# Attention's running state in half the columns, its products on quarters of the array, and one reciprocal square root for two layer norms, in a fused FFN, linear attention and FFN kernel

## The reference

```python
def _L0_attn_ref(x, Wqkv, bqkv, Wout, bout, gamma, beta):      # x is layer-normed
    q, k, v = jnp.split(x @ Wqkv.T + bqkv, 3, axis=-1)         # 16 heads of 16
    q = (jax.nn.elu(q) + 1.0 + FEAT_EPS) / jnp.sqrt(jnp.asarray(E, q.dtype))
    k = jax.nn.elu(k) + 1.0 + FEAT_EPS
    kv_cumsum = jnp.cumsum(jnp.einsum('blhe,blhf->blhef', k, v), axis=1)
    k_cumsum = jnp.cumsum(k, axis=1)
    num = jnp.einsum('blhe,blhef->blhf', q, kv_cumsum)
    den = jnp.einsum('blhe,blhe->blh', q, k_cumsum)[..., None] + FEAT_EPS
    out = (num / den).reshape(B, L, D) @ Wout.T + bout
    mu, var = jnp.mean(out, -1, keepdims=True), jnp.var(out, -1, keepdims=True)
    return (out - mu) / jnp.sqrt(var + LN_EPS) * gamma + beta
...
x = x + 0.5 * _L0_ffn_ref(_layernorm(x), w_gate, w_up, w_down)
x = x + _L0_attn_ref(_layernorm(x), ...)
x = x + 0.5 * _L0_ffn_ref(_layernorm(x), w_gate, w_up, w_down)
```

## Time and profile before

| | us |
|---|---|
| median of 3 runs (2298.89 to 2307.05) | 2300.2 |
| the profiled execution | 2303.45 |
| its span, first to last instruction | 2301.4 |
| PE busy, in the span | 2168.6 (94%) |
| DVE busy | 2135.8 (93%) |
| POOL busy | 1981.5 (86%) |
| ACT busy | 1853.5 (81%) |
| the causal mask of the first tile starts, that of the last | 802.2, 1560.4 |

### The profile page before, as it was taken

The page is one execution under the profiler, slowest core; times in us unless marked ns, Lnnn a source line. Parts: engine busy times, 40 slices in busy tenths (PEclk is TensorE's granted clock), DMA queues, the critical chain, the costliest instruction groups (busy, mean ns, idle before and its releaser), DMA issues.

```text
span 2301.4 us, 84889 instructions
## 1 busy us (share of the span) xinstructions
PE 2168.6 (94%) x27362; PEld 1558.6 (68%) x27362; DVE 2135.8 (93%) x5237; ACT 1853.5 (81%) x3878; POOL 1981.5 (86%) x3241
## 2 busy tenths in 40 slices
PE   0599999999999899999999999996999999999998
PEld 0356666666666689888889988883666666656665
DVE  8889999999999789999999999997999999999997
ACT  2778888888888678888888888877888888888885
POOL 1689999999999789998999999987989899899996
PEclk9899999999999999999999999998999999999999
DMA  3265555555554433333333333332544444444445
GB/s 93 54 125 111 118 111 117 112 116 112 116 115 97 87 63 69 69 68 67 68 69 66 69 68 68 67 66 46 109 116 112 110 115 111 115 112 108 117 111 118
DMA packets 733441, 216.28 MB, mean 94 GB/s; under 512 B 664774, under 2 KB 733126, under 8 KB 733382
## 3 DMA queue, kind: packets, MB, share of 16 engines
q1 hardware_dynamic: 733382, 215.57, 43.2%
HBM read 20.38 MB, written 16.78 MB: 16 GB/s over the span
## 4 chain that ended last, share of the span: by engine, by line
PE 39%; DVE 37%; issue 9%; POOL 8%; DVEq 2%; DMA 1%; SPq 1%; ACT 1%; POOLq 0%; ACTq 0%
DVE ffn_y L566 10%; DVE ffn_per_block L535 8%; PE attn_ps_qk L1068 7%; DVE ffn_hx L528 6%; PE ffn_ps_gu L676 6%; PE attn_ps_sc L1107 6%; POOL ffn_h_hl L609 3%; PE attn_ps_z L1129 3%; DVE ffn_q L562 3%; PE ffn_ps_down L688 3%; PE attn_ps_kT_v L1075 3%; PE attn_ps_num L1091 3%; PE attn_ps_num L1097 3%; POOL ffn_h_hl L608 3%; PE attn_ps_kv L1119 2%
## 5 line engine op out<-in xcount | busy, mean ns | idle before, releaser
L676 PE MATMUL ffn_ps_gu<-wgu_hi,ffn_xT 128*128 128x512 f16 (+1 forms) x3072 | 738.0, 363 | 32.7 <-DMA ffn_xT<-ffn_x_hl 32.7
L676 PEld LDWEIGHTS ffn_ps_gu<-wgu_hi,ffn_xT 128*128 128x128 f16 x3072 | 301.0, 98 | 319.2 <-issue 30.9
L676 PE MATMUL ffn_ps_gu<-wgu_lo,ffn_xT 128*128 128x512 f16 (+1 forms) x1536 | 431.9, 363 | 0.0
L624 ACT ACTIVATE ffn_quarter<-ffn_y,offsets 128x960 int16<-128x960 f32 (+2 forms) x264 | 282.6, 1071 | 172.9 <-DVE ffn_y L566 172.0
L688 PE MATMUL ffn_ps_down<-wd_hi,ffn_hT 128*128 128x256 f16 x2816 | 350.9, 273 | 19.9 <-DVE x_sb L555 13.9
L608 POOL TENSOR_TENSOR ffn_h_hl<-ffn_q,ffn_h_scale_hi 128x704 f16<-128x704 f16 x256 | 351.2, 1372 | 13.8 <-issue 6.3
L609 POOL TENSOR_TENSOR ffn_h_hl<-ffn_q,ffn_h_scale_lo 128x704 f16<-128x704 f16 x256 | 354.0, 1383 | 0.0
L688 PEld LDWEIGHTS ffn_ps_down<-wd_hi,ffn_hT 128*128 128x128 f16 x2816 | 265.5, 98 | 100.6 <-issue 36.9
L535 DVE TENSOR_REDUCE ffn_per_block<-ffn_hx 128x60 f32<-128x960 f32 (+2 forms) x264 | 298.5, 1131 | 22.7 <-ACT ffn_hx L660 0.3
L566 DVE TENSOR_TENSOR ffn_y<-ffn_hx,ffn_per_block 128x960 f32<-128x960 f32 (+2 forms) x264 | 295.4, 1119 | 0.0
L658 ACT ACTIVATE ffn_odd<-ffn_quarter,offsets 128x960 f16<-128x960 int16 (+2 forms) x264 | 278.6, 1055 | 5.5 <-POOL ffn_shift L601 5.5
(11 more groups left out here) (170 smaller groups left out, 5365.9 us busy)
## 6 DMA issues: line engine op xcount, KB each, us to landing
attn_v_eo<-attn_v_nat SPq DMA_DIRECT2D x512, 34.0 KB, 1.9
x_sb<-in_L_attn_x SPq DMA_DIRECT2D x128, 128.0 KB, 2.2
out<-x_sb SPq DMA_DIRECT2D x128, 128.0 KB, 1.8
ffn_xT<-ffn_x_hl SPq DMA_TRANSPOSE x256, 2.4
ffn_hT<-ffn_h_hl SPq DMA_TRANSPOSE x256, 3.5
attn_xT<-attn_x_hl SPq DMA_TRANSPOSE x128
attn_oT<-attn_o_hl SPq DMA_TRANSPOSE x128, 2.4
x_sb<-in_L_ffn_w_gate SPq DMA_DIRECT2D x1, 704.0 KB
```

What stands on the lines that cost most here:

```text
L624: nc.scalar.activation(quarter[:, back], y[:, back], ACT.Identity, bias=offsets[:, 0:1], scale=4.0 / HALF_MIN).then_inc(S["quarter"], 1)
L676: last = nc.tensor.matmul(ps_gu[par][:, a:b], xT[par][:, c, :], w[:, k, a:b], start=(n == 0), stop=(n == len(terms) - 1))
```

## The change

Five things change, all in attention.

1. **State.** The raw state is computed per 64 columns of k (g = 0, 1) with only the four heads of v that belong to them. Four heads' 17 columns stand in a row, 68 for each c, so `first`, `second`, `mid` and `before` have 136 columns where they had 272. `own` is the mask for that.
2. **PE's products.** q times state is done as 64x64 pieces of the array over 68 columns, after the products of the scores with v. The scores are done as 64x64 pieces too, twice as many with half the output rows. `ps_num` takes two banks (heads in the order of g), and the banks for k's transposes and v also hold the two raw states.
3. **Order on PE and ACT.** The transposes of k stand behind q and k's projection, and `k_nat` on ACT behind the exponential. The waits that this takes are new: v waits for `v_nat` and `second`, the raw state for `v_nat` of the next tile, `ps_num` for k's spread form and q's rows, which only the scores waited for.
4. **One square root.** The variances of x and z stand in one tile, so one addition and one power of two columns replace two of each. On POOL beta's sum and `shift` change places.
5. **Small.** o's scale goes into `den`, so `o` is a plain product of two tensors. The setup has 3 loads more on SP (`wout` in 4 pieces), and three small instructions more.

```diff
+        first, second = sb("first", [P, DC, PAIRS, VW]), sb("second", [P, DC, PAIRS, VW])
...
-        ps_kT_v = psum("ps_kT_v", [P, 512])
+        ps_kT_first = psum("ps_kT_first", [P, 512])
...
-        ps_kv = psum("ps_kv", [P, 2, 512])
-        ps_num = psum("ps_num", [P, HEADS, VW])
+        ps_v_second = psum("ps_v_second", [P, 512])
+        ps_num = psum("ps_num", [P, 2, 512])
...
-            return ps_kv[:, s, 0:HEADS * VW].rearrange("p (h w) -> p h w", w=VW)
+            return (ps_kT_first, ps_v_second)[s][:, D:D + WIDE]
...
-                nc.vector.tensor_scalar(den[:], ps_num[:, :, E], 4.0 * FEAT_EPS, None, ALU.add).then_inc(S["den"], 1)
+                nc.vector.tensor_scalar(den[:].rearrange("p (g h) -> p g h", g=2), num[:, :, :, E], 4.0 * FEAT_EPS, o_scale[:, 2:3], ALU.add, ALU.mult).then_inc(S["den"], 1)
...
-                nc.vector.scalar_tensor_tensor(o[:].rearrange("p (h e) -> p h e", e=E), ps_num[:, :, 0:E], o_scale[:, 0:1],
-                                               rden[:].unsqueeze(2).to_broadcast([P, HEADS, E]), ALU.mult, ALU.mult).then_inc(S["o_ready"], 1)
+                nc.vector.tensor_tensor(o[:].rearrange("p (g h e) -> p g h e", g=2, e=E), num[:, :, :, 0:E],
+                                        rden[:].rearrange("p (g h) -> p g h", g=2).unsqueeze(3).to_broadcast([P, 2, HEADS // 2, E]), ALU.mult).then_inc(S["o_ready"], 1)
...
-                ready(pool, "stats", tn)
-                freed(pool, "xn", tn, 2)
-                nc.gpsimd.tensor_tensor(rstd[oth][:], mv[oth][:, 1:2], eps[:], ALU.add).then_inc(S["var"], 1)
...
             if valid(tn, N):
-                ready(pool, "var", tn)
-                nc.gpsimd.tensor_tensor(rstd[oth][:], rstd[oth][:], minus_half[:], ALU.pow).then_inc(S["rstd"], 1)
+                ready(pool, "stats", tn)
+                freed(pool, "xn", tn, 2)
             if valid(tz, N):
                 ready(pool, "z_stats", tz)
                 if not (isinstance(tz, int) and tz < 2):
                     pool.wait_ge(attn_added, tz - 1)
+            if valid(tn, N) or valid(tz, N):
+                nc.gpsimd.tensor_tensor(rstd[oth][:, both], mv[oth][:].rearrange("p (s two) -> p s two", two=2)[:, both, 1], eps2[:, both], ALU.add).then_inc(S["var"], 1)
+                pool.wait_ge(S["var"], i + 4)
+                nc.gpsimd.tensor_tensor(rstd[oth][:, both], rstd[oth][:, both], minus_half[:, both], ALU.pow).then_inc(S["rstd"], 1)
             if valid(tn, N):
-                ready(pool, "rstd", tn)
-            if valid(tz, N):
-                nc.gpsimd.tensor_tensor(z_rstd[oth][:], z_mv[oth][:, 1:2], z_eps[:], ALU.add).then_inc(S["z_var"], 1)
-            if valid(tn, N):
-                nc.gpsimd.tensor_scalar(shift[oth][:], mv[oth][:, 0:1], -1.0, rstd[oth][:], ALU.mult, ALU.mult).then_inc(S["shift"], 1)
+                pool.wait_ge(S["rstd"], i + 4)
             if valid(tb, N):
                 nc.gpsimd.tensor_tensor(x_sb[:, tb, :], x_sb[:, tb, :], rows[:, 2, :], ALU.add).then_inc(S["x_beta"], 1)
-            if valid(tz, N):
-                ready(pool, "z_var", tz)
-                nc.gpsimd.tensor_tensor(z_rstd[oth][:], z_rstd[oth][:], minus_half[:], ALU.pow).then_inc(S["z_rstd"], 1)
+            if valid(tn, N):
+                nc.gpsimd.tensor_scalar(shift[oth][:], mv[oth][:, 0:1], -1.0, rstd[oth][:, 0:1], ALU.mult, ALU.mult).then_inc(S["shift"], 1)
...
+                nc.scalar.activation(k_nat[:], ps_kT, ACT.Identity, bias=feat_eps[:]).then_inc(S["k_nat"], 1)
...
+                freed(pe, "kv_first", i, 1)
...
-                    ready(pe, "k_nat", i)
+                    ready(pe, "v_nat", i)
+                    if not (isinstance(i, int) and i == 0):
+                        pe.wait_ge(S["kv_second"], i)
...
+            if valid(tn, N):
+                for c in range(DC):
+                    for r in range(PAIRS):
+                        for u in range(4):
+                            s, m = u // 2, u % 2
+                            h = c * PAIRS + r % 2 * 2
+                            nc.tensor.matmul(num[quarter(u), r // 2, h:h + 2, :], scores[:, r // 2, c, s, r % 2, quarter(m)], v_eo[oth][:, s, :, c * PAIRS + r, :],
+                                             start=(c == 0 and r % 2 == 0), stop=False, skip_group_check=True)
+                for c in range(DC):
+                    for s, st in enumerate((before, mid)):
+                        for g in range(2):
+                            last = nc.tensor.matmul(num[half(s), g, c * PAIRS:(c + 1) * PAIRS, :], q_feat[oth][half(g), c, half(s)], st[oth][half(g), c],
+                                                    start=False, stop=True, skip_group_check=True)
+                last.then_inc(S["num_done"], 1)
...
-                            last = nc.tensor.matmul(ps_sc[:, g, c, s], k_eo[par][half(g), c, s], q_rows[par][half(g), c, :, half(s)], start=True, stop=True)
+                        for a in range(2):
+                            for g in range(2):
+                                last = nc.tensor.matmul(ps_sc[half(a), g, c, s], k_eo[par][half(g), c, s, a], q_rows[par][half(g), c, :, half(s)], start=True, stop=True)
...
+                ready(pe, "v_nat", i + 1 if valid(tf, N) else i)
...
-                        own = v_nat[par][half(s), :, c * PAIRS:(c + 1) * PAIRS, :].rearrange("p a j w -> p j a w")
-                        last = nc.tensor.matmul(half_state(s)[:, c * 2 * PAIRS:(c + 1) * 2 * PAIRS, :].rearrange("p (j a) w -> p j a w", a=2),
-                                                k_nat[half(s), c * P:(c + 1) * P], own, start=True, stop=True)
+                    for g in range(2):
+                        for s in range(2):
+                            j = c * PAIRS + g * 2
+                            own_v = v_nat[par][half(s), :, j:j + 2, :].rearrange("p a j w -> p j a w")
+                            last = nc.tensor.matmul(half_state(s)[half(g), c * PAIRS * VW:(c + 1) * PAIRS * VW].rearrange("p (j a w) -> p j a w", a=2, w=VW),
+                                                    k_nat[half(s), c * P + g * SUB:c * P + (g + 1) * SUB], own_v, start=True, stop=True)
```

139 lines of the change are left out of this document (67 added, 72 removed).

## The result

| | before | after |
|---|---|---|
| median of 4 runs each, us | 2300.8 | 2379.1 |
| the profiled execution | 2303.5 | 2378.2 |
| its span | 2301.4 | 2376.5 |
| POOL busy in the span | 1981.5 | 1893.3 |
| DVE busy in the span | 2135.8 | 2107.9 |

The changed kernel is slower, 1.0334 of the time of before (95% interval 1.0312 to 1.0356), 78 us. The forecast was 2344, in a range of 2308 to 2385. The masks show where the time went: attention is 75.9 us longer; what lies ahead of the first mask is 0.7 longer and what lies behind the last start is 1.5 shorter. The medians of the kernel before moved between 2300.8 and 2305.6 from one set of runs to the next, so a difference of some 3 us between runs of different sets tells nothing.

The account below looks back on a forecast made before the run. POOL, in a ring with ACT, was taken to bound attention: its steps sum to 6.26 us a tile against 5.90, and 122 turns by 0.36 are 44 us, giving 2344 against the median 2300.2; range 2308 to 2385.

Parts of the forecast that it names:

- The ring: POOL and ACT: `shift`, `xn`, x's high half, POOL's low half; an unfilled wait makes 6.26 us a tile; chance 0.70.
- the sum of 6.26: POOL's start-to-start distances over one attention tile after the change, 6.26 us, where the same sum before gave 5.85.
- The second column: POOL's merged power: its second column taken at 0.05 us, between nothing and 0.36.
- the rival: POOL's power: the second column costs in full, 0.31 us more, 6.57 a tile, 2382 us; chance 0.07.
- `shift` to the low half: POOL, from `shift` to x's low half, waiting for ACT's high half: 1.53 us, as before the change.
- k's even form: POOL, k's form behind `mid`: start to start 0.57 us to the odd form, as before the change.
- `mid`: POOL's `mid` with 136 columns fewer: 0.46 us, between 0.38 and 0.60.
- DVE's part: DVE in attention: `first`, `second`, `before` save 0.42 us, `o` 0.07, `den` costs nothing; 5.41 a tile needed.
- the faster case: POOL's wait ahead of x's low half isn't there in full; DVE and PE set 5.41 us, 2240; chance 0.10.
- PE's part: PE in attention: `ps_num` 0.95 us saves 0.2, scores unchanged, raw state saves 0.23; about 5.4 a tile.
- Both PE rivals: PE's 64x64 pieces: quarters run only in pairs, 2434 us, chance 0.02; or start 46 ns apart, 2410, chance 0.03.
- The moved waits: Attention: moved `k_nat` and the raw state's new wait for `v_nat` cost nothing; `ps_num`'s new wait got no separate cost.

Follow-up runs that it names:

- run 1: Changed kernel with `shift` put ahead of beta's sum on POOL again, so that beta's sum lies in POOL's wait: 2308.2 us, ratio 1.0018.
- run 2: Kernel before the change with only beta's sum put ahead of `shift` on POOL: 2430.4 us, ratio 1.0545.
- run 3: Changed kernel with POOL's old order and its two additions and two powers again, all else as changed: 2304.4 us, ratio 1.0001.
- run 4: Changed kernel with a power of four columns in place of two, the extra pair unused: 2430.9 us, ratio 1.0551.
- run 8: Run 1's kernel with PE's waits for k's odd form, q's rows and the masked scores back at the scores: 2299.0 us, ratio 0.9976.
- run 9: Changed kernel with only PE's waits for k's odd form, q's rows and the masked scores back at the scores: 2403.8 us, ratio 1.0427.
- run 7: Run 3's kernel with PE's waits for k's odd form, q's rows and the masked scores back at the scores: 2273.6 us, ratio 0.9862.
- run 5: Run 1's kernel with x's low half a turn later, its transpose later too, and o's high half ahead of `xn` on ACT: 2316.2 us, ratio 1.0048.
- run 11: Run 5's kernel with PE's waits back at the scores and one input of `before` read from PSUM instead of SBUF: 2311.9 us, ratio 1.0033.

## Why the prediction was right, and what its sizes missed

- **The ring: right.** POOL idle "some 1.2 us a tile, ended by ACT's high half": 1.35. DVE's 0.8 idle: 0.81. PE waits for k's odd form, 1.12 a tile where 0.8 was foreseen. POOL is busy 71% of the 500 us, under the 80% named. Masks at 6.5 for 6.2 to 6.3. Runs 1 and 2 show the cause from both kernels, run 3 that undoing order and merge undoes the loss.
- **The step that was short is the sum of 6.26**; the trace has 6.51, 0.25 by 122 are 31 of the 34 us missed. Term by term, measured for forecast: `mid` to k's even form 0.57 for 0.56; even to odd **0.64 for 0.57**; odd to var 0.56 for 0.61; var 0.27 for 0.27; power with its wait and second column **0.89 for 0.77**; beta 0.71 for 0.69; `shift` to the low half **1.61 for 1.53**; the two low halves 1.26 for 1.26.
- **The second column** costs 0.15 (run 4), between the 0.05 taken and the 0.36 of the rival, and the wait for the power's result is 0.19 where 0.17 was taken. The prediction's own sign of being wrong, a power above 0.67, came true: 0.70. The argument from 272 columns of an addition doesn't carry to a power.
- **`shift` to the low half** was read from one tile, which gave 1.53. The distance changes from tile to tile (`xn` to its high half takes 0.63 there and 0.72 in the tile shown above); its mean over 900 to 1540 us is 1.60 before and 1.61 after. Nothing changed there: a mean should have been read, not a tile.
- **k's even form** was priced at its old length. In the trace after, it starts beside DVE's sum into x and takes 0.55 for 0.48. The prediction has no term for this.
- **`mid`** took 0.48 for 0.46. Its upper bound of 0.60 was called a third of the saving lost; with a third of 0.30 lost it is 0.56.
- **DVE's part: right in the parts, wrong in `before`.** `first` 0.29, `second` 0.35, `o` 0.42, as summed; `before` 0.54 for 0.35, beside k's odd form. `den`'s second operand, taken at nothing, costs 0.07 (0.23 for 0.17). It costs nothing while the ring binds, but DVE's "5.41" came out at 5.7 here (6.49 less the wait of 0.80), 5.5 in run 1 and 5.8 in run 8, and no run came near the 2240 of the faster case.
- **PE's part: right within 0.2.** Quarters of the array run side by side: 32 scores in 0.88 us are 28 ns each, and 16 of the raw state start within 0.20, 13 ns apart. Both PE rivals fell. By the Trainium skill, "TensorE: Matmul & The Clock Gate", section "Wait — 56ns, not 53.3ns?", matmuls start 25 ns apart at the least, by which the 16 would need 0.38 from first to last start, an estimate; the trace disagrees.
- **The moved waits: priced at nothing.** Wrong, and in both directions: in the changed kernel undoing them costs 21 to 25 us (run 9), with the ring gone it brings 31 (run 7). A wait doesn't only cost its length, it sets which instructions lie side by side. So that the time fell inside the range was partly luck: the same ring, with PE's waits at the scores, took 2403.8, and 2385 was the end of the range.

## What to carry to other kernels

Ahead of merging two instructions or moving one, look at what they fill: if the next instruction on the engine waits for another engine, the work removed or moved turns into idle time, and the engines that gained stand behind it. Two lines swapped decided 71 us here, and the best kernel with the merged power took 2299.0 (run 8). After the rings, lay POOL's and DVE's timelines over one another and check which DVE instructions with two SBUF inputs fall on which of POOL's; the best kernel (run 7) is the change without its merged power and without its moved wait.

## What the runs showed of the hardware

**A DVE instruction with two inputs in SBUF and a POOL instruction don't run together.** The one that starts later ends when the other has ended plus its own length, less 0.12 to 0.15 us with POOL the later and 0.20 to 0.21 with DVE. From the rows above, with POOL the later: run 2, 1206.55 + 0.48 = 1207.03, measured 1206.91; run 3, 1207.73 + 0.48 = 1208.21, measured 1208.06; run 9, o's low half, 1210.36 + 0.67 = 1211.03, measured 1210.90. With DVE the later: run 5, 1211.85 + 0.35 = 1212.20, measured 1212.00; run 7, 1211.52 + 0.48 = 1212.00, measured 1211.79; the changed kernel, `before`, 1207.72 + 0.35 = 1208.07, measured 1207.87. When the two start within some 0.05 us of each other the recorded starts don't tell the order: in run 8 the sum into x starts 0.02 ahead of `mid`, while o's low half still runs, and it is the sum that pays, 1206.59 + 0.48 = 1207.07, measured 1206.86. The profile shows no wait there, only a longer instruction, so it looks like work: in the kernel before, too, DVE's sum into x took 0.59 as a mean for its 0.48, and this is part of why DVE showed no gap there. With one input in PSUM nothing is held (run 11). The Trainium skill says the same, in "SBUF — State Buffer", section "Who interferes with whom": a DVE instruction with two SBUF inputs contends with one of POOL that reads SBUF, and the shared port pair is an exclusive lock, where the order of issue decides who blocks. The measurements agree, but for the 0.12 to 0.21 by which the two still overlap. The power is hardly touched: beside `before` it took 0.74 for 0.70 (run 1), and `before` its own 0.35.

**A power on POOL costs by the column.** 0.55, 0.70 and 1.02 us for one, two and four columns, where an addition takes 0.19 for one and for two.
